# The last 32 tokens of a pair first, as full fp32 products in four column strips, with the queues of all engines reordered

## The reference, cut to what matters

```python
x = x + _L0_conv_ref(_ln_c(x), ...)      # spatial gate, then channel gate, then the residual
...
router_probs = softmax(x @ router_w + router_b)          # 8 experts
top_p, top_i = top_k(router_probs, 2); top_p = top_p / sum(top_p)
expert_out = einsum('bnd,edc->bnec', x, expert_w) + expert_b
gathered = take_along_axis(expert_out, top_i[..., None], axis=2)
return einsum('bnk,bnkc->bnc', top_p, gathered)
```

## Time and profile before

| what | value |
|---|---|
| median of three runs | 1960.88 us (1959.79 to 1966.5) |
| profiled execution, its own time | 1958.27 us |
| its span | 1956.5 us |
| TensorE (PE) busy | 1779.4 us, 91% |
| VectorE (DVE) busy | 1502.8 us, 77% |
| ScalarE (ACT) busy | 1195.2 us, 61% |
| GpSimd (POOL) busy | 1131.6 us, 58% |
| moved by DMA | 135.13 MB |

### The profile page before, as it was taken

One profiled execution on the slowest core, in us unless ns is written; L12 is line 12 of the kernel. 1 busy time (PEld: TensorE's weight loads), 2 busy tenths in 40 slices (PEclk: granted clock), 3 DMA queues, 4 the chain that ended last, 5 costly groups with the idle time before them and its releaser, 6 DMA issues.

```text
span 1956.5 us, 38711 instructions
## 1 busy us (share of the span) xinstructions
PE 1779.4 (91%) x13076; PEld 1301.2 (67%) x13076; DVE 1502.8 (77%) x4703; ACT 1195.2 (61%) x3346; POOL 1131.6 (58%) x1268
## 2 busy tenths in 40 slices
PE   4889999999999999999999999999999999998996
PEld 3467667667666666666766766666766676666764
DVE  4458778788777788777778877778877778877666
ACT  3446656566666666665656665666666666666554
POOL 1134557575556666556666555667555666655565
PEclk9799999999999999999999999999999999999998
DMA  4111121212222211222121222121222221121111
GB/s 126 50 67 51 67 84 67 75 57 70 77 74 70 81 59 67 76 67 84 67 70 57 75 67 83 67 84 51 76 73 70 74 77 62 64 75 51 50 51 50
DMA packets 56177, 135.13 MB, mean 69 GB/s; under 512 B 16268, under 2 KB 18333, under 8 KB 55982
## 3 DMA queue, kind: packets, MB, share of 16 engines
q1 hardware_dynamic: 55320, 130.81, 19.6%
q10 hardware_dynamic: 662, 1.84, 0.3%
HBM read 106.50 MB, written 26.13 MB: 68 GB/s over the span
## 4 chain that ended last, share of the span: by engine, by line
PE 47%; POOL 29%; ACT 13%; DVE 6%; issue 4%; DMA 1%; SPq 0%; POOLq 0%; ACTq 0%; DVEq 0%
POOL part L559 8%; ACT part L795 7%; POOL x1l L544 6%; POOL rstd L508 5%; POOL otok L564 5%; DVE part L1663 4%; PE high L1233 3%; PE high L1235 3%; PE high L1234 3%; PE rot L1056 3%; PE rot L1043 3%; PE rot L1186 2%; PE low L1233 2%; PE rot L1057 2%; ACT tok L646 2%
## 5 line engine op out<-in xcount | busy, mean ns | idle before, releaser
L559 POOL TENSOR_TENSOR part<-part 128x256 f32<-128x256 f32 (+1 forms) x416 | 332.0, 798 | 445.8 <-DVE part L1663 445.7
L795 ACT ACTIVATE part<-low,gv 128x128 f32<-128x128 f32 (+1 forms) x1664 | 460.1, 393 | 164.8 <-PE low L1235 81.6
L1663 DVE SCALAR_TENSOR_TENSOR part<-high,gv,part 128x128 f32<-128x128 f32 (+1 forms) x1664 | 452.1, 339 | 122.3 <-ACT part L795 100.0
L1087 PE MATMUL rot<-x1h,wch 128*128 128x256 f32 x960 | 237.3, 287 | 0.0
L564 POOL TENSOR_TENSOR otok<-part 128x128 f32<-128x128 f32 (+1 forms) x416 | 212.8, 512 | 32.6
L1088 PE MATMUL rot<-x1h,wcl 128*128 128x256 f32 x960 | 228.3, 278 | 0.0
L526 POOL TENSOR_TENSOR tp_l<-tp,tp_h 128x448 fp32r<-128x448 f32 x64 | 66.1, 1032 | 247.5 <-ACT tp_h L675 245.0
L1087 PEld LDWEIGHTS rot<-x1h,wch 128*128 128x128 f32 x960 | 180.9, 188 | 10.0 <-issue 9.4
L1233 PE MATMUL high<-weh,xh 128*128 128x512 f32 (+1 forms) x416 | 178.4, 429 | 8.6 <-DVE part L1663 8.5
L1233 PE MATMUL low<-weh,xh 128*128 128x512 f32 (+1 forms) x416 | 179.1, 431 | 3.5 <-ACT part L795 3.2
L1088 PEld LDWEIGHTS rot<-x1h,wcl 128*128 128x128 f32 x960 | 181.1, 189 | 0.1
(11 more groups left out here) (242 smaller groups left out, 4072.2 us busy)
## 6 DMA issues: line engine op xcount, KB each, us to landing
xin<-in_x SPq DMA_DIRECT2D x32, 784.0 KB, 4.3
x<-in_x SPq DMA_DIRECT2D x32, 784.0 KB, 4.4
cen<-shift_rows SPq DMA_DIRECT2D x32, 784.0 KB, 4.3
out<-x SPq DMA_DIRECT2D x64, 392.0 KB, 2.4
y_ch<-rstd_rows SPq DMA_DIRECT2D x32, 768.0 KB, 3.8
otok<-in_ggs_w SPq DMA_DIRECT2D x1, 600.2 KB
tok<-in_ggs_w SPq DMA_DIRECT2D x1, 600.2 KB
rstd_rows<-both_rows SPq DMA_DIRECT2D x32, 7.0 KB
```

The costliest lines, as they stand in the source:

```text
L559: nc.gpsimd.tensor_tensor(part[0:n, slot, 0:2, :], part[0:n, slot, 0:2, :], part[0:n, slot, 2:4, :], ALU.add).then_inc(sem("half_sum"), 1)
L795: last = nc.scalar.activation(part[0:n, turn % RING, e, :], low[turn % 2][0:n, e * C:(e + 1) * C], ACT.Copy, scale=gv[par(p, back)][0:n, i ...
L1087: nc.tensor.matmul(dst, wch[:, j, rows], hi_x, start=(j == 0), stop=False)
L1663: last = nc.vector.scalar_tensor_tensor(out=own, in0=high[turn % 2][0:n, e * C:(e + 1) * C], scalar=gv[par(p, back)][0:n, i, HALF + e:HALF ...
```

## The change

Three things are changed.

1. **The 32 tokens beyond the twelve full tiles come first.** `tile(i)` maps turn 0 to the thirteenth tile and turn i to tile i - 1. In turn 0 `rest_products` takes the place of `products`: eight fp32 matmuls with the 32 centred tokens of `cen` as the stationary operand and 256 columns (two experts) of the weights streaming, in four strips of 32 partitions of one `low` bank, first with `weh` and then with `wel`. The eight experts of the 32 tokens stand in that one bank, so turn 0 uses no `high` bank, and both `gate_low(0)` and `gate_high(0)` read the `low` bank; `low_half(2)` waits for both. `x_high` and `x_low` no longer split the 32 tokens (four pieces of 384 columns each).
2. **The lists of all engines and `USES` are written in another order.** Among it: `finish(0)` moves from `back` 5 to the end of the step with `back` 4, `space_logit` and the first two `x2_tokens` move from the end of a step to the start of the next, the rest tokens' products and one more low half stand near the router, and `normalise` is spread between the gates.
3. On SyncE, `rstd_out` and `rstd_in` are issued ahead of the second image's store and of `load_residual`, and `shift_in` waits for the rest products too, since they read `cen`.

```diff
+        def tile(i):
+
+            return (i + TILES - 1) % TILES
+
+        def rest(v, e):
+
+            return v[32 * (e // 2):32 * (e // 2) + PAIR * S % 128, (e % 2) * C:(e % 2 + 1) * C]
...
                         need(sp, "logit_filled", k, p, 1, back + 1)
...
@@ -457,10 +466,10 @@
                 shift_out(4)
                 shift_in(4)
                 store(0, 5)
+                rstd_out(1)
+                rstd_in(1)
                 store(1, 5)
                 load_residual(3)
-                rstd_out(1)
-                rstd_in(1)
                 load(0)
                 if 2 * k + p == 1:
...
+                            src = rest(low[turn % 2], e) if i == 0 else low[turn % 2][:, e * C:(e + 1) * C]
+                            last = nc.scalar.activation(part[0:n, turn % RING, e, :], src, ACT.Copy,
+                                                        scale=gv[par(p, back)][0:n, t, e:e + 1])
...
+                def rest_products(dst):
+                    for n, w in enumerate((weh, wel)):
+                        for g in range(4):
+                            last = nc.tensor.matmul(dst[32 * g:32 * g + 32, 0:2 * C], flat(cen)[:, 128 * (TILES - 1):PAIR * S],
+                                                    w[:, 2 * g:2 * g + 2, :].rearrange("p e c -> p (e c)").bitcast(F32),
+                                                    start=(n == 0), stop=(n == 1))
+                    return last
...
-                        tile_ready(i, back)
                         need(pe, "low_gated", k, p, m + 1, mb)
-                        products(low[count_of(k, p, back, i) % 2], i, slice(0, HALF), back).then_inc(sem("low_filled"), 1)
+                        if m == 0:
+                            need(pe, "high_gated", k, p, 1, mb)
+                        dst = low[count_of(k, p, back, i) % 2]
+                        if i == 0:
+                            need(pe, "centred_ready", k, p, 4, back)
+                            rest_products(dst).then_inc(sem("low_filled"), 1)
+                        else:
+                            tile_ready(tile(i), back)
+                            products(dst, tile(i), slice(0, HALF), back).then_inc(sem("low_filled"), 1)
...
+                        m, mb = (i - 2, back) if i > 2 else (i + TILES - 3, back + 1)
                         need(pe, "high_gated", k, p, m + 1, mb)
-                        products(high[count_of(k, p, back, i) % 2], i, slice(HALF, E), back).then_inc(sem("high_filled"), 1)
+                        tile_ready(tile(i), back)
+                        products(high[i % 2], tile(i), slice(HALF, E), back).then_inc(sem("high_filled"), 1)
...
                         for e in range(HALF):
                             own = part[0:n, turn % RING, e, :]
+                            src = high[i % 2][:, e * C:(e + 1) * C] if i else rest(low[turn % 2], HALF + e)
                             last = nc.vector.scalar_tensor_tensor(
-                                out=own, in0=high[turn % 2][0:n, e * C:(e + 1) * C],
-                                scalar=gv[par(p, back)][0:n, i, HALF + e:HALF + e + 1], in1=own, op0=ALU.mult, op1=ALU.add)
```

Of the lists, the last third of TensorE's shows the pattern:

```diff
+                high_half(9, 5)
+                high_half(10, 5)
                 if 2 * k + p == 3:
                     expert_weights()
                 channels0_high(3)
+                finish(1, 5)
+                low_half(11, 5)
+                low_half(12, 5)
+                channels0_low(3)
                 high_half(11, 5)
                 high_half(12, 5)
-                channels0_low(3)
+                joint(0, 0, 2)
                 finish(2, 5)
                 channels(1, 3)
+                rstd_turn(1)
                 logits(4)
-                joint(0, 0, 2)
-                finish(3, 5)
+                low_half(0, 4)
                 gram_first(3)
                 router(4)
+                low_half(1, 4)
+                gram_turn(3)
+                finish(3, 5)
                 channels(2, 3)
-                rstd_turn(1)
-                gram_turn(3)
-                high_half(0, 4)
-                high_half(1, 4)
                 joint_c(3)
                 joint(0, 1, 2)
                 hidden_c(3)
-                low_half(0, 4)
-                low_half(1, 4)
+                high_half(1, 4)
+                high_half(2, 4)
                 channel_logit(3)
+                hidden(0, 2)
                 joint(1, 0, 2)
-                x1_channels(0, 0, 3)
                 low_half(2, 4)
                 low_half(3, 4)
-                high_half(2, 4)
                 high_half(3, 4)
+                x1_channels(0, 0, 3)
+                joint(1, 1, 2)
+                x1_channels(0, 1, 3)
                 low_half(4, 4)
                 low_half(5, 4)
                 high_half(4, 4)
                 high_half(5, 4)
+                x1_channels(1, 0, 3)
+                hidden(1, 2)
                 low_half(6, 4)
-                x2_tokens(0, 3)
-                joint(1, 1, 2)
-                hidden(0, 2)
-                hidden(1, 2)
-                x1_channels(0, 1, 3)
-                x1_channels(1, 0, 3)
```

235 lines of the change are left out of this document (118 added, 117 removed).

## The result

The changed kernel takes 1819.01 us (median of four runs, 1818.09 to 1823.65); the kernel before takes 1961.86 in the runs beside it. The ratio is 0.9274, with a 95% interval of 0.925 to 0.9297. The forecast was 1847 us with a range of 1828 to 1902. The direction and the mechanism were right. The forecast gain was too small: between the profiled spans it is 1956.5 - 1816.3 = 140.2 us where the sum had 111, and the time lies 9 us beyond the fast end of the range. Three terms of the sum failed: 3 us for the steps outside the steady ones (14.7 came), 0.3 us a step for stops that remain (none did), and 0.4 us a step of TensorE's work saved (0.66 came).

What follows compares the result with a forecast made beforehand. A loop through four engines' queues was taken to bound the step; 3.8 us of stops and 0.4 of products, less 0.3 for remaining stops, gave 54.0 us a step. 108 us over 28 steps plus 3 made 1958.3 - 111 = 1847 us, range 1828 to 1902.

Steps and rivals of the forecast that it cites:

- The bound and the mechanism: A loop through four engines' queues sets the step; the new order removes TensorE's stops, 3.8 us a step.
- The rest products: Eight fp32 matmuls on TensorE take 1.0 us in place of two halves' 1.40, saving 0.40 us a step.
- The walk: New lists laid out by profiled durations, asking whether each TensorE piece finds input and bank ready; no late wait found.
- margin of 0.1 us: Before the logits on TensorE: `cen` complete at 29.9, logits due at 30.0 us.
- stops that go, a step: TensorE's waits, mainly before the logits and `finish(3)`, all go: 3.8 us a step.
- allowance for stops that remain: 0.3 us a step left for TensorE stops, since margins of 0.1 to 0.5 us match the walk's accuracy.
- outside the 28 steps: In some 335 us before and after the steady steps, only 3 us gained, from first steps with products.
- better than forecast: Rival: no stop at all and outer steps gain too, 53.6 us a step, 10 us outside, 1830 us; chance 0.07.
- stop stayed before the logits or `gram_first`: Rival: 1 to 3 us a step of stop come back on TensorE, 1903 us (1875 to 1931); chance 0.21.
- The strips: Rival: the rest products' four strips don't run side by side, 3.8 us, step 56.8, 1925 us; chance 0.01.
- `normalise` ahead of the gates: Rival: late y rows stop VectorE's gates, about 2005 us at a landing of 46; slower or no gain, chance 0.05.
- What would show it: Profile signs: cadence near 54 us, `cen` and `otok` waits under 0.5, rest matmuls 0.95 to 1.25, VectorE 86% busy.

Runs made afterwards that it cites:

- e3: Changed kernel with the eight rest matmuls done a second time, same result: 1848.93 us, ratio 0.9433, 54.37 us a step.
- e12: Changed kernel with GpSimd's list as before the change, all else changed: 1942.43 us, ratio 0.9898, 57.38 us a step.
- e10: Changed kernel with a full fp32 copy of the expert weights, so four rest matmuls instead of eight: 1823.05 us, ratio 0.9291.
- e2: Kernel before with the new lists and `USES` but the old products, `high_half(0, 4)` kept: 1935.14 us, ratio 0.9864.
- e1: Kernel before with the changed rest products and turn numbering, every list and `USES` as before: 2026.99 us, ratio 1.0339.
- e9: Changed kernel with an extra small GpSimd sum between `inverse_std1` and the sum of turn 10: 1824.35 us, ratio 0.9311.
- e4: Changed kernel with VectorE's second `centre_tokens` and `finish(2)` put ahead of `centre`: 1847.15 us, ratio 0.9421.
- e8: Kernel before with `finish(3)` behind `gram_turn` and `channels(2)` on TensorE, VectorE, ScalarE and `USES` made to fit: 1951.9 us, ratio 0.9952.
- e5: e2 with the high half of turn 2 moved behind `low_half(3, 4)` on TensorE: 1854.15 us, ratio 0.9446, 54.38 us a step.

## Why the prediction was right in kind and short in size

**The bound and the mechanism** hold. The stops were 3.83 of the 4.48 us a step, and the new order takes all of them away. TensorE has no idle time in the 28 steps, e3 shows that work added to it is paid in full, and e12 shows that this holds only while GpSimd's queue keeps its new order. A loop through VectorE lies close behind (e10).

**The rest products**: forecast 1.0 us between 0.94 and 1.28, measured 0.98. Right, and the mix's row in the profile was the better guide. What the walk did not see is their second effect: by using no `high` bank they take a wait of 1.73 us off `high_half(2)` (e2), and in e1 they move every sum by one turn. Products and order need each other.

**The walk.** The step "the pieces' durations in my walk are those measured while both engines ran, contended already" failed. The forecast took 3.33 us for `centre` and 2.70 for `moments1`; they took 1.98 and 2.42 (1039.71 to 1042.13 in the timeline of VectorE). The contention is no property of an instruction; it depends on what the other engine has under way, and a new order draws that anew. But e9 says how little hangs on it: with the slow `centre` the logits still had 0.75 us. So the margin of 0.1 us was too small by 2.0. The pace of `centre` is 1.35 of it, and `moments1`, `mix_low` and the first `centre_tokens` are 0.28, 0.34 and 0.24 us shorter than in the walk, which is together 0.2 more than the whole; the rest of the walk was that much too early. For `finish(3)` the walk was right: its last sum ends at 1052.39 and it starts at 1053.91, a margin of 1.5 us where the walk had 1.6.

**The sum, term by term.** 111 us were forecast and 140.2 came.

| term | forecast | measured | us |
|---|---|---|---|
| stops that go, a step | 3.8 | 3.83 | +0.8 |
| TensorE's work saved, a step | 0.4 | 0.66 | +7.2 |
| rounding: 57.85 less 53.7, where 3.8 and 0.4 make 4.2 | 4.15 a step | 4.2 | +1.4 |
| allowance for stops that remain | 0.3 a step | 0 | +8.4 |
| outside the 28 steps | 3 us | 14.7 us | +11.7 |

Together they are 29.5 us, which is the error (29.2) but for rounding. The largest term had no row behind it: "I count nothing but 3 us from the first steps". The first, last and unsteady steps run the same new order, so they gain as well: 6.0 us up to the first `inverse_std2`, 4.3 in the next interval, 4.3 at the end. In the kernel before, 14 transposes of `x_tokens` (75.91 us, 3.22) stand ahead of the first mix, which starts at 82.86, and the preparation of the weights follows it. In the changed kernel the mix starts at 78.36, 4.5 us earlier. The mix and that preparation, before and after, in the view of windows:

```profile
82.86:92.33 9.47, 9.47 (x64) 4.30 (x64) 0.00 (x0) 1.58 (x4) 4.45 (x4) 0.69 0.01 2
```

```profile
78.36:85.03 6.67, 6.67 (x65) 2.90 (x65) 0.00 (x0) 3.47 (x7) 4.51 (x4) 1.00 0.01 2
```

The same work takes 2.8 us less at the higher clock. From there to `inverse_std2` the changed kernel takes 36.23 us at 0.95 and the kernel before 34.93 at 0.99, so 1.3 us are given back: 4.5 + 2.8 - 1.3 = 6.0. This start is not steady: kernels with nearly the same lists have the first `inverse_std2` at 121.59 (e4), 123.69 (e9) and 125.22 us (e3), and e8, with nearly the lists of before, has it at 124.34. So up to 4 us of the 6.0 may be the chance of one execution.

The allowance was a judgement on margins that were computed with the slow durations of the kernel before. Of the 0.66 us of work, e5 gives 0.44 to the products, near the 0.40 of the forecast, and 0.21 to the order, for which the sum had nothing. The average from unit 0 holds one interval of 52.94 us, which was not steady (58.03 from unit 1 on); since the gain was added up from stops and work, this cost the forecast no more than the rounding in the table. The rival "better than forecast" named just this case, no stop and gains outside, at 1830 us, with a chance of 0.07 and still 10 us outside instead of 14.7. That chance was too low: every margin of the walk was positive, and nothing in the profile said that more stops must stay.

**The other rivals.** No stop stayed before the logits or `gram_first`. The strips run side by side: e3 has 0.43 us for a round of four, where the rival's 3.8 us for the two rounds would be 1.9. By the 2.38x for three column tiles in the Trainium skill, "TensorE: Matmul & The Clock Gate", section "Measured speedup vs the span model", the two rounds were 1.2 us as an estimate; 0.98 was measured with the surroundings and 0.86 without, so the measurement decides against it here. `normalise` ahead of the gates cost nothing: VectorE has no wait on the y rows from 900 to 1115 us.

**What would show it.** A cadence near 54: 53.55. Waits on `cen` and `otok` under 0.5 us: none. Rest products 0.95 to 1.25: 0.98. VectorE busy for 86% of a step: 44.45 / 53.59 = 83%, less because its instructions became shorter.

## What to carry to other kernels

If a walk through the queues finds every wait early, forecast the bound engine's own time as the step and put the doubt into the range; take the cadence from steps that are all steady, and count the gain of the outer steps too. Durations of VectorE and GpSimd that run beside each other don't carry over to another order: work them out at both paces, and ask whether the conclusion stands at the slow one. When one stop is undone, look first at what the edit itself puts late (e8). And read the granted clock behind a stop: part of what a stop costs can stand there and not in the list of waits (e1, e12).

## What the runs showed of the hardware

- A run of VectorE's two-input fp32 instructions and a sum on GpSimd share something. If no sum is under way when the run begins, VectorE's pieces take 0.50 us and a sum that begins just behind is held, 3.09 us in the changed kernel; if one is, VectorE's take 0.83 us and GpSimd's sums 0.66 to 1.29. e9 has both within one kernel, 11 and 21 times. This can change within a run (in e1 the fourth piece alone took 1.40 us), and what decides it then is open. The Trainium skill, "GPSIMD Engine Reference", section "Key points", says that the two share interfaces; the runs agree, and show that the split is not fixed.
- A stop of TensorE can cost more than its length. After the stop of 3.7 us in e1 the granted clock was 0.69 in the next 5 us, after one of 1.77 in e2 0.79 from 1069 to 1074, and e12's step at 0.97 takes 1.77 us more of TensorE's work than its step at 1.00. Not every stop does this: in the kernel before, after stops of 1.68 and 1.58 us, the clock from 1075 to 1080 us is 1.00.
- The fp32 matmuls of 256 columns in four strips cost 0.43 us a round of four, at a granted clock of 1.00 (e3).
